# Attention with masked keys on one Trainium2 core: the row maximum carried by a row of ones, the context loaded in a second layout, and 17 zero matmuls at the start

## The reference

```
xn  = layernorm(x)                          # over the 256 positions
qk  = einsum('bhdq,bhdl->bhql', xn, ctx) / 4
att = einsum('bhql,bhdl->bhdq', softmax(qk), ctx)
x   = x + tanh(g_xattn) * gamma * att
h   = layernorm(x)
x   = x + tanh(g_ffn) * (silu(h @ e4m3(gate_w) * gs) * (h @ e4m3(up_w) * us)) @ e4m3(down_w) * ds
```

## Time and profile before

| what | value |
|---|---|
| median of three runs | 215.9 us (215.54 to 220.35) |
| the profiled execution's own time | 215.64 us, span 213.8 us |
| PE busy | 197.2 us, 92% of the span |
| DVE busy | 158.8 us, 74% |
| POOL busy | 146.5 us, 68% |
| ACT busy | 124.8 us, 58% |
| attention phase, first P to twelfth P | 28.99 to 107.46 us |
| last P (end of attention) | starts 141.39 us |

### The profile page before, as it was taken

How to read it: one execution, slowest core, us unless ns; L and a number is a source line. 1 busy time by engine, 2 the same in 40 slices (tenths; PEclk the granted TensorE clock), 3 DMA queues, 4 the chain that set the end, 5 groups by cost and what they waited for, 6 DMA issues and landing times.

```text
span 213.8 us, 4671 instructions
## 1 busy us (share of the span) xinstructions
PE 197.2 (92%) x1760; PEld 118.5 (55%) x1760; DVE 158.8 (74%) x335; ACT 124.8 (58%) x242; POOL 146.5 (68%) x167
## 2 busy tenths in 40 slices
PE   0669999999999999999999988999899999999991
PEld 0225556655665566556655553446666666766581
DVE  3499999989999997688967715053956677765985
ACT  2011858776877586768675864278627644854450
POOL 5992879967999999973799203372564799567440
PEclk9999999999999999999999998899999999999999
DMA  6799501101131231132311312211330002003022
GB/s 190 225 352 386 99 5 52 30 24 51 52 102 58 69 120 37 47 120 74 104 49 53 103 61 68 76 52 49 104 108 0 2 0 98 3 0 98 5 98 98
DMA packets 19783, 17.75 MB, mean 83 GB/s; under 512 B 4016, under 2 KB 19248, under 8 KB 19760
## 3 DMA queue, kind: packets, MB, share of 16 engines
q1 hardware_dynamic: 19760, 17.44, 26.3%
HBM read 11.02 MB, written 6.42 MB: 82 GB/s over the span
## 4 chain that ended last, share of the span: by engine, by line
PE 79%; DVE 11%; ACT 3%; issue 3%; POOL 1%; DMA 1%; SPq 0%; DVEq 0%; ACTq 0%; POOLq 0%
PE ps L723 19%; PE ps L787 17%; PE ps L764 13%; PE ps L735 12%; PE ps L845 9%; DVE neg_max L542 5%; PE ps L738 4%; PE ps L751 2%; PE ps L748 2%; ACT p_t L465 1%; DMA c_sb<-in_ctx 1%; PE ps L774 1%; ACT xn L494 1%; DVE p_t L697 1%; DVE p_t L692 1%
## 5 line engine op out<-in xcount | busy, mean ns | idle before, releaser
L542 DVE TENSOR_REDUCE neg_max<-ps 128x2 f32<-128x512 f32 x128 | 79.4, 681 | 13.3 <-PE ps L723 13.1
L723 PE MATMUL ps<-km,qn 32*128 32x512 f32 x256 | 76.9, 693 | 8.3 <-POOL qn L348 7.7
L465 ACT ACTIVATE p_t<-ps 128x512 f32<-128x512 f32 x128 | 66.8, 599 | 22.4 <-PE ps L738 20.5
L735 PE MATMUL ps<-qm,c_sb 32*128 32x512 f32 x256 | 74.9, 651 | 1.3 <-ACT p_t L465 1.3
L787 PE MATMUL ps<-w_exp,w_gu 128*128 128x512 f16 x192 | 46.6, 388 | 1.3 <-DVE w_exp L593 1.3
L431 POOL TENSOR_TENSOR f_lo<-fu,f_hi 128x512 fp32r<-128x512 f32 x23 | 29.4, 1280 | 22.9 <-ACT f_hi L483 22.9
L738 PE MATMUL ps<-max_t,sel 4*128 4x256 bf16 x256 | 35.1, 273 | 0.0
L723 PEld LDWEIGHTS ps<-km,qn 32*128 32x128 f32 x256 | 26.1, 204 | 14.2 <-issue 14.2
L658 DVE SCALAR_TENSOR_TENSOR ga<-th,ps 128x512 f32<-128x512 f32 x24 | 16.3, 681 | 21.2 <-ACT th L478 21.2
L738 PEld LDWEIGHTS ps<-max_t,sel 4*128 4x128 bf16 x256 | 18.9, 96 | 23.1 <-issue 20.7
L764 PE MATMUL ps<-p_t,v_t 128*32 128x256 f32 x512 | 30.9, 382 | 0.4 <-ACT p_t L465 0.4
(11 more groups left out here) (66 smaller groups left out, 218.8 us busy)
## 6 DMA issues: line engine op xcount, KB each, us to landing
u_scr<-u_sb SPq DMA_DIRECT2D x32, 128.0 KB
u_n<-u_scr SPq DMA_DIRECT2D x16, 128.0 KB
r_n<-r_scr SPq DMA_DIRECT2D x16, 128.0 KB
out_x<-p_t SPq DMA_DIRECT2D x16, 128.0 KB, 1.8
x_sb<-in_x SPq DMA_DIRECT2D x3, 512.0 KB, 8.1
c_sb<-in_ctx SPq DMA_DIRECT2D x3, 512.0 KB, 8.7
w_all<-in_L_ffn_gate_w SPq DMA_DIRECT2D x1, 768.0 KB, 9.3
w_all<-in_L_ffn_up_w SPq DMA_DIRECT2D x1, 768.0 KB, 9.8
```

Of the source, the lines that this page charges most:

```text
L465: nc.scalar.activation(p_t[:, b % 2, i, :], ps[:, bank_of["t", n][0], :], ACT.Exp, scale=DH ** -0.5).then_inc(exp_ok, 1)
L542: nc.vector.tensor_reduce(neg_max[:, b % 2, at:at + PAR, 0], ps[:, bank_of["s", n][0], :].rearrange("p (e l) -> p e l", e=PAR), axis=AX.X, ...
L723: nc.tensor.matmul(ps[:, bank, :], qn[rows, b % 2, P * t:P * (t + 1)], km[rows, b % 2].rearrange("p e l -> p (e l)"), start=True, stop=Tru ...
L735: nc.tensor.matmul(ps[:, bank, :], c_sb[rows, b, P * t:P * (t + 1)], qm[rows, b % 4].rearrange("p e l -> p (e l)"), start=True, stop=False)
```

## The change

It has these parts:
- **Masked keys with a row of ones** (`keys`): where the other head's features were zeroed, one row is now 1. The negated maximum then rides in the matching row of the queries, and t needs no separate product for it: L738 goes. t reads `km` as its weights, once per head: two products of 256 columns in place of one of 512. `km` has 4 buffers (2 before).
- **The maximum without a split**: `reduce_max` writes into a float32 tile `nm`; T is two float32 transposes of it. `split_max` goes. VectorE builds `qm` from T's bank and `qn` (`shifted_queries`), in place of GpSimd's two multiplications and ScalarE's `max_out`.
- **The context in rows**: a second input, `ctx_t`, the transposed context, is loaded by DMA (2 MB more), and GpSimd copies it to `v_t` (`context`), in place of two transposes and ScalarE's `v_out`.
- **GpSimd's forms**: `km` is now a multiply and an add with two scalars per partition; `qn` adds a negated mean, which is one more small operation per group of batches, in place of subtracting the mean. The second half of `binades` (maximum and multiply) moves from VectorE to GpSimd; the steps in which the halves are done move too. The keys of batch 0 are made by VectorE.
- **TensorE's order**: `STEP`, `ASIDE` and `turn`'s place. T now stands apart from P, after the third s of the step.
- **17 zero matmuls** of 256 columns in bf16 stand before everything on TensorE.

The diff, cut to its core:

```diff
-ASIDE = 1
+ASIDE = 2
 RING = 8
-STEP = "stssttttssPTststst"
-ROWS = 4
+STEP = "ststtssTststPststt"
...
-HALF_BINADES = (1, 2, 4, 5, 6, 8)
-HALF_ROUNDED = (2, 3, 5, 6, 7, 8)
+HALF_BINADES = (1, 2, 4, 6, 8, 10)
+HALF_ROUNDED = (2, 4, 6, 8, 10, 11)
...
+            def load_context(n):
+                lo, hi = GROUPS[n]
+                if n >= 3:
+                    sp.wait_ge(vt_sb, hi - 8)
+                sp.dma_start(ct_sb[:, lo % 8:lo % 8 + hi - lo], ctx_t[lo:hi].rearrange("b (t p) d -> p b t d", p=P)
+                             ).then_inc(ct_in[n], 16)
...
+                if n < 3:
+                    load_context(n)
...
+                if b in (3, 7):
+                    load_context(3 + b // CH)
...
+                nc.gpsimd.tensor_scalar(neg_m[:, lo:hi], mv[:, lo:hi, 0], -1.0, None, ALU.mult).then_inc(r1_ok, 1)
...
             def keys(b):
-                pool.wait_ge(masks_ok, 1)
+                pool.wait_ge(masks_ok, 3)
                 pool.wait_ge(c_in[group_of(b)], 16)
-                if b >= 2:
-                    pool.wait_ge(max_ok, FILLS * (b - 1))
-                for e in range(PAR):
-                    nc.gpsimd.tensor_scalar(km[:, b % 2, e, :], c_sb[:, b, :], mask[:, e:e + 1], 1.0,
-                                            ALU.mult, ALU.mult).then_inc(k_ok, 1)
-
-            def queries(b):
-                pool.wait_ge(r1_ok, group_of(b) + 1)
-                if b >= 2:
-                    pool.wait_ge(max_ok, FILLS * (b - 1))
-                nc.gpsimd.tensor_scalar(qn[:, b % 2, :], x_sb[:, b, :], mv[:, b, 0:1], rstd[:, b:b + 1],
-                                        ALU.subtract, ALU.mult).then_inc(qn_ok, 1)
                 if b >= 4:
                     pool.wait_ge(exp_ok, FILLS * (b - 3))
-                pool.wait_ge(qn_ok, b + 1)
-                for e in range(PAR):
-                    nc.gpsimd.tensor_scalar(qm[:, b % 4, e, :], qn[:, b % 2, :], mask[:, e:e + 1], 1.0,
-                                            ALU.mult, ALU.mult).then_inc(qm_ok, 1)
-
-            keys(0)
+                for s in range(PAR):
+                    nc.gpsimd.tensor_scalar(km[:, b % 4, s, :], c_sb[:, b, :], mask[:, 1 - s:2 - s], one[:, s:s + 1],
+                                            ALU.mult, ALU.add).then_inc(k_ok, 1)
+
+            def queries(b):
+                pool.wait_ge(r1_ok, 2 * group_of(b) + 2)
+                if b >= 3:
+                    pool.wait_ge(qm_ok, PAR * (b - 2))
+                nc.gpsimd.tensor_scalar(qn[:, b % 3, :], x_sb[:, b, :], neg_m[:, b:b + 1], rstd[:, b:b + 1],
+                                        ALU.add, ALU.mult).then_inc(qn_ok, 1)
...
+                nc.gpsimd.tensor_scalar(exp, exp, E4M3_MIN_EXP, E4M3_MAGIC, ALU.max, ALU.mult).then_inc(w_mag, 1)
+                pool.wait_ge(w_mag, k + 1)
...
-                    nc.gpsimd.tensor_scalar(xn2[:, q, :], x_sb[:, t, :], mv2[:, t, 0:1], rstd2[:, t:t + 1],
-                                            ALU.subtract, ALU.mult).then_inc(n2_ok, 1)
-
+                    nc.gpsimd.tensor_scalar(xn2[:, q, :], x_sb[:, t, :], neg_m2[:, t:t + 1], rstd2[:, t:t + 1],
+                                            ALU.add, ALU.mult).then_inc(n2_ok, 1)
+
+            def context(b):
+                pool.wait_ge(ct_in[group_of(b)], 16)
+                if b >= 3:
+                    pool.wait_ge(pv_ok, b - 2)
+                nc.gpsimd.tensor_copy(v_t[:, b % 3, :, :, 1:1 + DH],
+                                      ct_sb[:, b % 8].rearrange("p t (h d) -> p t h d", h=NH)).then_inc(vt_sb, 1)
...
+                if b + 1 < NB:
+                    context(b + 1)
...
-                    if i == 4 and b + 1 < NB:
-                        max_out(b + 1)
-                        v_out(b + 1)
...
-                nc.vector.tensor_reduce(neg_max[:, b % 2, at:at + PAR, 0],
+                if b >= 2:
+                    v.wait_ge(m_ok, b - 1)
+                to = nm[:, b % 2, t, :].rearrange("p (g s r) -> p g s r", g=NG, s=PAR)
+                nc.vector.tensor_reduce(to[:, g, :, 0],
...
-            def split_max(b):
...
-                    nc.vector.tensor_reduce(high, pair[:, :, :, 0:1], axis=AX.X, op=ALU.max).then_inc(mx_hi, 1)
...
-                    nc.vector.tensor_reduce(low, pair, axis=AX.X, op=ALU.add).then_inc(mx_ok, 1)
...
+            def shifted_queries(b):
+                v.wait_ge(m_ok, b + 1)
+                v.wait_ge(qn_ok, b + 1)
+                if b >= 2:
+                    v.wait_ge(exp_ok, FILLS * (b - 1))
+                for e in range(PAR):
+                    nc.vector.scalar_tensor_tensor(qm[:, b % 2, e, :], ps[:, bank_of["T", b][0], 0:L],
+                                                   mask[:, 1 - e:2 - e], qn[:, b % 3, :],
+                                                   ALU.mult, ALU.add).then_inc(qm_ok, 1)
...
-                                        ALU.bitwise_and).then_inc(w_and, 1)
-                v.wait_ge(w_and, k + 1)
-                nc.vector.tensor_scalar(exp, exp, E4M3_MIN_EXP, E4M3_MAGIC,
-                                        ALU.max, ALU.mult).then_inc(w_exp_ok, 1)
+                                        ALU.bitwise_and).then_inc(w_exp_ok, 1)
...
+            v.wait_ge(c_in[0], 16)
+            for s in range(PAR):
+                nc.vector.tensor_scalar(km[:, 0, s, :], c_sb[:, 0, :], mask[:, 1 - s:2 - s], one[:, s:s + 1],
+                                        ALU.mult, ALU.add).then_inc(k0_ok, 1)
...
-                if b in (0, 3, 7):
-                    stats_group({0: 2, 3: 3, 7: 4}[b])
+                if b in (1, 3, 7):
+                    stats_group({1: 2, 3: 3, 7: 4}[b])
...
-                    if i == 0 and b > 1:
-                        split_max(b - 1)
-                    if i == 3 and b > 0:
+                    if i == 2 and b > 0:
+                        shifted_queries(b - 1)
+                    if i == 4 and b > 0:
                         between(b - 1)
-                if b in (0, NB - 1):
-                    split_max(b)
+            shifted_queries(NB - 1)
...
-                    pe.wait_ge(mt_sb, held[1] + 1)
-                    pe.wait_ge(vt_sb, held[1] + 1)
+                    pe.wait_ge(qm_ok, PAR * (held[1] + 1))
...
-                rows, head = slice(SLOTW * g, SLOTW * (g + 1)), slice(SLOTW * g, SLOTW * g + ROWS)
-                nc.tensor.matmul(ps[:, bank, :], c_sb[rows, b, P * t:P * (t + 1)],
-                                 qm[rows, b % 4].rearrange("p e l -> p (e l)"), start=True, stop=False)
+                rows = slice(SLOTW * g, SLOTW * (g + 1))
                 for e in range(PAR):
-                    last = nc.tensor.matmul(ps[:, bank, L * e:L * (e + 1)], sel[head, e, :], max_t[head, b % 2, :],
-                                            start=False, stop=(e == PAR - 1))
+                    last = nc.tensor.matmul(ps[:, bank, L * e:L * (e + 1)], km[rows, b % 4, 1 - e, P * t:P * (t + 1)],
+                                            qm[rows, b % 2, e, :], start=True, stop=True)
...
             def turn(b):
-                pe.wait_ge(mx_ok, b + 1)
-                pe.wait_ge(c_in[group_of(b)], 16)
+                pe.wait_ge(max_ok, FILLS * (b + 1))
                 bank, held = bank_of["T", b]
                 bank_free(held)
                 for t in range(LT):
-                    nc.tensor.matmul(ps[:, bank, P * t:P * (t + 1)], nm_parts[:, t, :], ident_b[:],
-                                     start=True, stop=True)
-                for t in range(LT):
-                    last = nc.tensor.transpose(ps[:, bank, L + P * t:L + P * (t + 1)], c_sb[:, b, P * t:P * (t + 1)],
-                                               ident[:])
+                    last = nc.tensor.transpose(ps[:, bank, P * t:P * (t + 1)], nm[:, b % 2, t, :], ident[:])
...
+            pe.wait_ge(idle_ok, 1)
+            for _ in range(17):
+                nc.tensor.matmul(ps[:, RING - 1, 0:L], idle[:, 0:P], idle[:, 0:L], start=True, stop=True)
...
+        if name == "ctx_2048":
+            a = np.ascontiguousarray(a.transpose(0, 2, 1))
+            arrays["in_ctx_t"] = a
+            args.append(nc.dram_tensor("in_ctx_t", a.shape, mybir.dt.from_np(a.dtype), kind="ExternalInput").ap())
```

More of the change, by code:

```diff
@@ L64, in bank_table, with build @@
     return table, held
-def build(nc, x, ctx, g_xattn, g_ffn, gamma, gate_w, up_w, down_w, gate_scale, up_scale, down_scale, out):
+def build(nc, x, ctx, ctx_t, g_xattn, g_ffn, gamma, gate_w, up_w, down_w, gate_scale, up_scale, down_scale, out):
     f32, f32r, bf16, f16, u32 = (mybir.dt.float32, mybir.dt.float32r, mybir.dt.bfloat16,
@@ L89, in build @@
         ident = sb("ident", [P, P])
-        ident_b = sb("ident_b", [P, P], bf16)
-        ones_b = sb("ones_b", [P, P], bf16)
         mask = sb("mask", [P, PAR])
-        pick = sb("pick", [P, PAR])
-        sel = sb("sel", [P, PAR, P], bf16)
+        one = sb("one", [P, PAR])
         mhalf = sb("mhalf", [P, CH])
@@ L99, in build @@
```

(26 more changed lines are left out.)

88 lines of the change are left out of this document (31 added, 57 removed).

## The result

| | before | changed |
|---|---|---|
| median | 215.72 us (215.26 to 220.35, 4 runs) | 218.31 us (216.79 to 222.06, 4 runs) |
| profiled execution: own time, span | 215.64, 213.8 us | 217.2, 215.4 us |
| first P, twelfth P, last P start | 28.91, 107.45, 141.39 us | 28.34, 113.22, 142.99 us |

The ratio is 1.0108, interval [1.0063, 1.0153]: a loss clear of noise, though under 2%; 210.0 us was forecast. Some executions of any of these kernels are over 1.5% longer than its fastest; the ratios leave them out, the medians don't. (The P's are given from here on by their first matmul; the chain of the earlier trace rows counts from 0.08 us later.)

The account below looks back on a forecast made before the run. TensorE, busy 92% of the span, was taken to bound the kernel. From 215.64 us the prediction took 2.8 for the eleven steps, 1.7 for the start and 1.1 for the end, giving 210.0; range 206 to 222.

Parts of the forecast that it names:

- the start: Up to the first P: earlier first s and first t, of which 1.7 us counted, bounds 0.8 and 3.
- the end: Last rounds of t without L738: 0.2 us less in each of five, 0.1 for T, 1.1 us saved.
- the choice between the bounds: GpSimd's `km` and `qn` with two scalars: 0.48 us each taken, between a lower 0.48 and upper 1.24.
- The added loads of t: TensorE, four loads per t in place of two: hidden, zero cost taken; upper bound 0.64 us a step.
- the steps together: Eleven steps, first to twelfth P: 11 x 6.3 + 4.4 + 2 = 75.7 us, against 78.5.
- the quiet step: TensorE step between P's: 6.3 us, with T starting 3.1 us after P's end, 0.4 lost waiting for its maximum.
- the statistics: VectorE, three times between first and twelfth P: 1.2 us each, reciprocals 0.8 with the third, 4.4 us added.
- the waits on PSUM banks: TensorE waiting on P's bank, which ScalarE read late: 0.8 us a step, said to go with the new order.
- GpSimd, 2 us said: Steps 8 to 11: GpSimd's work 28.9 us against 25.2, partly covered by its lead, so 2 us show.
- the price of the maximum-and-multiply: GpSimd operation over 768 elements per half weight: 1.3 us taken, range 1.3 to 3.7.
- a lead of 1.5 us: GpSimd ahead of TensorE by some 1.5 us before steps 8 to 11, covering part of its excess work.
- rival 2: GpSimd becomes the bound: 225 us through dear `km` and `qn`, 218 if only the maximum-and-multiply, both 239; chance 0.17.

Follow-up runs that it names:

- experiment 4: Changed kernel with `qn` on GpSimd subtracting the mean again, still with two scalars; one run, 228.22 us.
- experiment 9: Changed kernel with the maximum in GpSimd's 768-element operation replaced by a multiplication by 1; one run, 211.62 us.
- experiment 1: Changed kernel with the context copy for batch b issued in GpSimd's turn b, not b-1; 213.31 us, ratio 0.989 to the kernel before.
- Experiment 12: Kernel of experiment 10 with GpSimd's 768-element pair in the other order, multiply then maximum; 211.52 us.
- experiment 10: Changed kernel with context copy in its own turn, statistics one batch a step, small scalings on ScalarE and GpSimd, weight halves never in neighbouring turns; 209.91 us.

## Why the prediction was wrong

The forecast was 210.0, the profiled execution took 217.2: 9.2 us of the difference stand in the eleven steps and 1.1 at the start, and the end gives 3.1 back.

**What held.** The first s came at 5.83 (5.4 said) and the first t at 14.54 (14.5). `km` and `qn` cost 0.556 and 0.554 (0.48), and experiment 4 shows that the choice between the bounds was right for the right reason. The added loads of t are hidden, as the earlier trace rows had it: in the quiet step its passes of 256 columns follow each other on a row group every 0.21 us. The trace does not agree here with the Trainium skill's rule that the prediction cites (TensorE: Matmul & The Clock Gate, section Part 3), by which loads on the same row group would show. The product of `qm` costs 0.476 (0.48).

**Where it failed: the steps together, 75.7 us said, 84.9 measured, 9.2 too few.** Two terms make it, the quiet step with a wait for a PSUM bank that the prediction put at nothing (6.4), and GpSimd (5.3); the statistics went the other way (2.5).

1. *The quiet step, 6.88 in place of 6.3: 11 x 0.58 = 6.4 us.* Timeline of the step from 57.31, TensorE and then VectorE:

```profile
57.31 1.93 PE L752 MATMUL ps<-p_t,v_t 128*32 128x256 f32 x32
...
61.69 0.70 PE L719 MATMUL ps<-km,qn 32*128 32x512 f32 x2
...
62.22 0.59 PE L719 MATMUL ps<-km,qn 32*128 32x512 f32 x2
62.74 0.44 PE L740 MATMUL ps<-ident,nm 128*128 128x128 f32 x2
```
```profile
60.34 3.79 DVE L542 TENSOR_REDUCE nm<-ps 128x2 f32<-128x512 f32 x6 [0.64 <-PE ps L719]
```

The first maximum starts 1.16 us after P's end, as worked out. But the third pair of products isn't free to go then: it needs the bank that the second maximum gives back at 60.34 + 0.60 + 0.68 = 61.62. It starts at 61.69, its second pass streams to 62.22 + 0.43 = 62.65, and T, on the full array, comes behind them: 3.56 us after P's end, not 3.1. I had asked only for T's own semaphore. The four products after T take 1.08 with their entry, not 0.95. This term holds in every kernel with the new order: in none of their profiled executions is a step between the first and the twelfth P under 6.87 us. It alone puts the forecast at 216.4, and so takes the whole forecast gain. The prediction had said of the waits on PSUM banks that they go with the new order; one came in their place, on the second maximum's bank, that sets T back by 0.46 us. No experiment moved T or the ring, so this stands on the timeline and on the order of the program.

2. *GpSimd, 2 us said.* The statistics are charged with the steps that stay longer in experiment 9, where little waits for GpSimd: 7.25, 8.00 and 7.25, so 1.87 us over three quiet steps, where 4.4 was said. (VectorE's spare time covers more than was thought.) Of the 9.2 us by which the changed kernel's eleven steps exceed 11 x 6.88, some 7.3 are left for GpSimd's lateness and the low clock behind it, 5.3 more than said. The step that failed here is the price of the maximum-and-multiply: 1.3 was taken because `km` at 0.48 per 256 elements seemed the general form, with 3.7 as upper bound; 2.78 was measured. In steps 8 to 11 alone that is 3 x 1.48 = 4.4 us more. The wait of the copy on P was overlooked altogether: I counted on GpSimd's busy time and a lead of 1.5 us, and a queue that waits in order has no lead. Experiments 1 and 9 show that it takes both: without the wait the span is 211.6 us, without the maximum 209.8.

*The start*: 1.7 us said at the first P, 0.6 measured. Of the lead of 2.7 us at the first t, 2.1 are lost again. VectorE is busy 9.34 of 10.20 us in the stretch of low clock (11.0 to 21.2), and by experiment 1 it is VectorE that sets the first P, with the clock worth 0.4 us. *The end*: 1.1 said, 4.2 measured over the last four steps. Experiment 12 prices the low stretch there at 12.12 - 10.47 = 1.65 us; the kernel before has a low stretch there and the changed one hasn't. An estimate of what the change itself gives is then 4.2 - 1.65, about 2.5 us, against 1.1; no run separates it.

**Set against rival 2** (GpSimd becomes the bound; 218 us, if only the maximum-and-multiply were dear): that is the case that came, at 218.3, though by 2.78 and the copy's wait together, and not by 3.7. That the number fits is luck: the 218 was 210 and 8 us of GpSimd, and measured are 216.4 by the quiet step, then some 5 more of GpSimd, less what statistics and the end gave. It is luck too that experiment 10, with 209.9, lands on the forecast: its eleven steps take 77.1 us, not 75.7. The rival's chance was set too low, by weighing the price with `km` as the nearest row: two prices in one form of instruction, 0.48 and 1.24, were a sign that the operation decides, and none of the rows showed a maximum on GpSimd. With six of them, and a place in the program where GpSimd already was over its budget, 0.17 was too little. The parts of the change that made the order (`STEP`, `ASIDE`, T's place) were never tried one by one.
